# Two attention layers with a bidirectional recurrence: the steps of the recurrence split into five parts and placed by a table

## The reference

```python
x = x + L0_attn(L0_cond(x, fside, fside, w, u, cond), W, g1, g2, g3)
x = x + L0_ffn(L0_cond2(x, fside, fside, w, u, cond), weight, bias)
x = x + L1_attn(L1_cond(x, fside, fside, w, u, cond), w_q, w_k, w_v, w_o)
x = x + L1_ffn(L1_cond2(x, fside, fside, w, u, cond), w1, w2)
```

```python
score = softmax(att, axis=-1) + softmax(att, axis=-2)
```

## Time and profile before

| | us |
|---|---|
| three runs: lowest, median, highest | 426.21, 428.22, 430.42 |
| the profiled execution: its time, and its span | 429.75, 428.0 |
| busy in the span: PE, DVE, ACT, POOL | 275.2, 262.7, 204.8, 47.1 |

### The profile page before, as it was taken

How to read it: one execution, slowest core, us unless ns; L and a number is a source line. 1 busy time by engine, 2 the same in 40 slices (tenths; PEclk the granted TensorE clock), 3 DMA queues, 4 the chain that set the end, 5 groups by cost and what they waited for, 6 DMA issues and landing times.

```text
span 428.0 us, 5935 instructions
## 1 busy us (share of the span) xinstructions
PE 275.2 (64%) x2278; PEld 170.7 (40%) x2278; DVE 262.7 (61%) x502; ACT 204.8 (48%) x333; POOL 47.1 (11%) x76
## 2 busy tenths in 40 slices
PE   0151866694696786737335428898889999755644
PEld 0141433462453353523212314665566666423413
DVE  2977976969669552698858354345456140494762
ACT  3655693865856735412650361551644343233512
POOL 2000111101111100053210502002000000000000
PEclk9996895896987788666658556898985865886986
DMA  5813554333765522022270500000000000000100
GB/s 172 331 31 70 99 100 80 70 74 75 165 131 98 102 50 51 0 49 49 51 147 0 98 0 0 2 2 0 2 2 0 2 2 0 0 2 1 49 27 25
DMA packets 8525, 23.58 MB, mean 55 GB/s; under 512 B 1585, under 2 KB 2993, under 8 KB 8113
## 3 DMA queue, kind: packets, MB, share of 16 engines
q0 software_dynamic: 4320, 15.73, 19.5%
q1 hardware_dynamic: 4176, 7.48, 5.1%
HBM read 6.43 MB, written 1.05 MB: 17 GB/s over the span
## 4 chain that ended last, share of the span: by engine, by line
PE 44%; DVE 27%; ACT 12%; issue 10%; DMA 4%; POOL 2%; DVEq 0%; ACTq 0%; POOLq 0%
PE PS L1224 7%; DVE fwd L649 5%; PE PO L1072 5%; PE PM L1172 4%; PE PM L1112 4%; PE PO L1057 4%; PE PO L1239 3%; PE PM L1028 3%; PE PM L1098 2%; DVE fwd L918 2%; DMA fwd<-mid 2%; DMA fwd<-bwd 2%; DVE bwd L657 2%; PE PM L1181 2%; DVE kp L873 2%
## 5 line engine op out<-in xcount | busy, mean ns | idle before, releaser
L873 DVE TENSOR_REDUCE kp<-PS 128x2 f32<-128x256 f32 x64 | 32.3, 551 | 25.5 <-PE PS L1203 25.4
L558 ACT ACTIVATE E<-PS 128x384 f32<-128x384 f32 x64 | 27.9, 490 | 37.1 <-PE PS L1224 37.0
L482 ACT ACTIVATE E<-PS,negc,escale 128x1024 f32<-128x1024 f32 x32 | 38.3, 1198 | 11.6 <-PE PS L1042 11.4
L1072 PE MATMUL PO<-E,vr 128*32 128x256 f32 x256 | 22.7, 483 | 32.7 <-DVE vr L751 26.4
L1002 PE MATMUL PM<-w,sg 128*128 128x256 f32 x32 | 11.3, 517 | 28.5 <-DVE sg L672 28.5
L460 ACT ACTIVATE yc<-PO 128x256 f32<-128x256 f32 x32 | 12.4, 387 | 30.5 <-PE PO L1057 29.1
L276 POOL DMA_DIRECT2D fwd<-mid x15 | 13.1, 872 | 122.0 <-DVE fwd L649 122.0
L1224 PE MATMUL PS<-TP 32*128 32x256 f32 (+1 forms) x128 | 20.2, 417 | 9.3 <-DVE kp L873 6.0
L1172 PE MATMUL PM<-G,sg 128*128 128x512 f32 x32 | 21.8, 842 | 6.6 <-DVE sg L672 6.5
L1072 PEld LDWEIGHTS PO<-E,vr 128*32 128x32 f32 x256 | 8.0, 126 | 41.5 <-DVE vr L751 37.2
L1028 PE MATMUL PM<-ident,kp 128*128 128x128 f32 x96 | 17.5, 341 | 10.9 <-POOL kp L341 8.8
(11 more groups left out here) (167 smaller groups left out, 626.2 us busy)
## 6 DMA issues: line engine op xcount, KB each, us to landing
fwd<-mid POOLq DMA_DIRECT2D x15, 512.0 KB, 4.5
fwd<-bwd POOLq DMA_DIRECT2D x15, 512.0 KB, 4.5
G<-in_w SPq DMA_DIRECT2D x2, 1024.0 KB, 9.6
kT<-in_kT SPq DMA_DIRECT2D x4, 256.0 KB, 6.6
xT<-in_xT SPq DMA_DIRECT2D x4, 256.0 KB, 6.2
G<-in_attn SPq DMA_DIRECT2D x1, 1024.0 KB, 6.4
out<-ek SPq DMA_DIRECT2D x8, 128.0 KB, 1.7
w<-in_attn SPq DMA_DIRECT2D x1, 512.0 KB, 7.5
```

Of the source, the lines that this page charges most:

```text
L482: nc.scalar.activation(E[:, p % 6], PS[:, 2 * (p % 2):2 * (p % 2) + 2, :], ACT.Exp, bias=negc[:], scale=escale[:]).then_inc(S["e0_done"], 1)
L558: nc.scalar.activation(E[:, p % 4, i, 0:384], PS[:, i, 0:384], ACT.Exp, scale=QSCALE).then_inc(S["e1_done"], 1)
L873: nc.vector.tensor_reduce(kp[:, b % 2, u * H + 2 * j:u * H + 2 * j + 2, D], PS[:, at0:at0 + 2, lo:hi], AX, ALU.max, negate=True).then_inc( ...
L1072: ins = nc.tensor.matmul(PO[SLOT * g:SLOT * (g + 1), 1, at:at + T], vr[:, q % 2, v * 4 + g, :], E[:, (2 * q + g // 2) % 6, g % 2, v * T:(v ...
```

## The change

- **Parts by a table.** Steps 2 to 11 are cut into five parts (`inputs`, two `ahead`, two `behind`), and a slot takes as many parts as `FILL` says, (2, 2, 2, 2, 1, 2, 1, 1) over eight slots. `prepare` is placed two slots before the first part, `wkv` three and `gate` four slots after the last. All ten steps end in slot 29, as they did.
- **Links higher.** `links` comes right after the first part of its slot; in slot 33, where there is none, before `gate(11)`.
- **Preparation of a batch** goes by a small table `PREP`, which differs for batch 1 alone: `project0(1)` moves from slot 1 to slot 2, the rest with it. `turn_y` moves up in its slot.
- **Late steps.** 14 and 15 move on: the parts of step 14 stand at slots -10 (`inputs`), -9 (`ahead`), -7 (`behind`), 5 (`wkv`), 7 (`gate`), those of step 15 at -2, 1, 3, 10 and 12. Step 13 keeps its scans; its `wkv`, with that of step 12, goes from slot -9 to -3. Each late `wkv` is behind a load of the table with the logarithm, and the next tanh loads the other.
- **Ternary weights.** They are loaded a second time, into `ek` and `ekv`, once all scans are done; rounding is in slots 14 and 22 and clipping in slots 16 and 24 of the second attention.
- **Clears.** The clear of `vt` on GpSimd moves to the start of the program, the large one of `kp` to VectorE in slot 34; the small ones stay on GpSimd, now before `add_mid(12)`.
- `cond` is loaded ahead of the first segment of `kT`; `prepare(12)` and `inputs(12)` are in slot 34, ahead of `yT_copy` and of three `gated`.

```diff
-        w1f = G[3][:, :]
-        w2f = G[2][:, :]
+        w1f = ek[:, :]
+        w2f = ekv[:, :]
...
-        M_AT = {n: 3 * (n - RAMP) for n in range(RAMP, BEFORE)}
-        M_AT[BEFORE] = B * PAIRS + 4
-        M_LATE = {BEFORE + i: -17 + 3 * i for i in range(1, B)}
+        FILL = (2, 2, 2, 2, 1, 2, 1, 1)
+        PART_AT = {}
+        for at in range(B * PAIRS):
+            for _ in range(FILL[at % PAIRS]):
+                n, part = divmod(len(PART_AT), 5)
+                if n + RAMP < BEFORE:
+                    PART_AT[n + RAMP, part] = at
+        LATE = {BEFORE + 1: (-14, -13, -12, -3, -1), BEFORE + 2: (-10, -9, -7, 5, 7),
+                BEFORE + 3: (-2, 1, 3, 10, 12)}
+        PREP = {1: 1, 2: PAIRS, 3: 2 * PAIRS}
...
+            sp.wait_ge(S["scan_done"], 4 * LAYERS * B)
+            sp.wait_ge(S["m_done"], LAYERS * B)
+            sp.dma_start(w1f, w1_d).then_inc(S["ld_w1"], 16)
+            sp.dma_start(w2f, w2_d).then_inc(S["ld_w2"], 16)
...
-            pool.wait_ge(S["ktr0_done"], HALF * B)
-            pool.wait_ge(S["y0_done"], B * CH)
-            nc.gpsimd.memset(vt[:, :, :, D:2 * D], 1.0).then_inc(S["v_ones"], 1)
+            pool.wait_ge(S["kp_clear"], 1)
-            link(nc.gpsimd.memset(kp[:, :, :, D:SLOT], 0.0))
...
-                for n in steps0(p, 0):
-                    inputs(n)
-                for n in steps0(p, 1):
-                    if n < BEFORE:
-                        ahead(n, 0)
-                        ahead(n, 1)
-                for n in steps0(p, 2):
-                    if n < BEFORE:
-                        behind(n, 0)
-                        behind(n, 1)
+                for i, (n, part) in enumerate(parts(p)):
+                    if part == 0:
+                        inputs(n)
+                    elif part <= 2:
+                        ahead(n, part - 1)
+                    else:
+                        behind(n, part - 3)
+                    if i == 0 and p % 2 == 1 and 0 <= (p - 3) // 2 < B * CH:
+                        links((p - 3) // 2)
...
+                if p == 34:
+                    dve.wait_ge(S["ktr0_done"], HALF * B)
+                    dve.wait_ge(S["vcols_done"], B * CH)
+                    nc.vector.memset(kp[:, :, :, D:SLOT], 0.0).then_inc(S["kp_clear"], 1)
+                    inputs(BEFORE)
+                    for bb in range(B - 1):
+                        gated(1, bb)
+                        largest(bb)
```

More of the change, by code:

```diff
@@ L197, in build, with parts, steps0, steps1 @@
         BEFORE = 3 * LAYERS
-        LAST = LAYERS * B - 1
-        M_AT = {n: 3 * (n - RAMP) for n in range(RAMP, BEFORE)}
-        M_AT[BEFORE] = B * PAIRS + 4
-        M_LATE = {BEFORE + i: -17 + 3 * i for i in range(1, B)}
-        def steps1(p, lag):
-            return [n for n, at in M_LATE.items() if at + lag == p]
-        def steps0(p, lag):
-            return [n for n, at in M_AT.items() if at + lag == p]
+        FILL = (2, 2, 2, 2, 1, 2, 1, 1)
[8 more added lines that the diff above has]
+        PREP = {1: 1, 2: PAIRS, 3: 2 * PAIRS}
+        def parts(p):
+            return [key for key, at in PART_AT.items() if at == p]
+        def steps0(p, part, lag):
+            return [n for n in range(RAMP, BEFORE) if PART_AT[n, part] + lag == p]
+        def steps1(p, i, lag=0):
+            return [n for n, at in LATE.items() if at[i] + lag == p]
+        def prep(p, lag):
+            return [b for b, at in PREP.items() if at + lag == p]
         def added(n):
@@ L230, in _ @@
         def _(sp):
+            sp.dma_start(cond[:], cond_d.partition_broadcast(P)).then_inc(S["ld_cond"], 16)
             sp.dma_start(kT[:, seg(0)], kT_d[:, seg(0)]).then_inc(S["ld_k0"], 16)
[L232 removed]
             sp.dma_start(vec[:], vec_d).then_inc(S["ld_vec"], 16)
@@ L324, in _ @@
                 link(nc.gpsimd.memset(kp[half[0], :, u * H:(u + 1) * H, at:at + 1], 1.0))
+            add_mid(BEFORE)
             add_back(BEFORE)
@@ L327, in _ @@
                 b, j = p // PAIRS + 2, p % PAIRS
-                for n in steps1(p, 1):
+                for n in steps1(p, 1, 1):
                     add_mid(n)
-                for n in steps1(p, 2):
+                for n in steps1(p, 2, 1):
                     add_back(n)
@@ L486, in _ @@
                     weight_abs(1)
[L487 to L490 removed]
                 if p % 2 == 0 and 0 <= p // 2 - 1 < B * CH:
                     rows_copy(p // 2 - 1, 0, "pv0_done", "turned0_done", "rows0_done")
+                for bb in prep(p, 1):
+                    square0(bb)
+                for bb in prep(p, 3):
+                    rms(bb)
                 if j == 3 and 1 <= b <= B:
                     yT_copy(b - 1, "ytr0_done", "out0_done", "yT0_done", gv[:])
[L495 to L498 removed]
+                for bb in prep(p, 5):
+                    kT_copy(bb, 0)
+                for bb in prep(p, 6):
+                    kT_copy(bb, 1)
                 if p % 4 == 3 and p >= 7 and (p - 7) // 4 < B * HALF:
                     turned_copy((p - 7) // 4)
[L501 to L509 removed]
+                for n in steps0(p, 4, 3):
+                    wkv(n)
+                for n in steps0(p, 0, -2):
+                    prepare(n)
+                if p == 34:
                     for bb in range(B - 1):
                         tanh(1, bb)
+                    prepare(BEFORE)
             tanh(1, B - 1)
@@ L734, in _ @@
             behind(1, 0)
+            behind(1, 1)
             low_parts(0, 0)
-            behind(1, 1)
             low_parts(0, 1)
@@ L800, in _ @@
-                if p == 0:
-                    gate(1)
-                for n in steps0(p, 6):
-                    if n < BEFORE:
-                        gate(n)
-                if j == 0 and b + 1 < B:
-                    gated(0, b + 1)
-                if j == 6 and b + 1 < B:
-                    low_parts(b + 1, 0)
-                if j == 7 and b + 1 < B:
-                    low_parts(b + 1, 1)
-                if p % 2 == 1 and 0 <= (p - 3) // 2 < B * CH:
-                    links((p - 3) // 2)
@@ L813, in _ @@
-                if j == 2 and b + 1 < B:
-                    sums0(b + 1)
-                if p == 34:
-                    for bb in range(B - 1):
-                        gated(1, bb)
-                        largest(bb)
+                for bb in prep(p, 4):
+                    normed(bb)
+                for i, (n, part) in enumerate(parts(p)):
[7 more added lines that the diff above has]
+                        links((p - 3) // 2)
@@ new lines, in _ @@
+                if not parts(p) and p % 2 == 1 and 0 <= (p - 3) // 2 < B * CH:
+                    links((p - 3) // 2)
+                if p == 1:
+                    gate(1)
+                for n in steps0(p, 4, 4):
+                    gate(n)
+                for bb in prep(p, 0):
+                    gated(0, bb)
+                for bb in prep(p, 6):
+                    low_parts(bb, 0)
+                for bb in prep(p, 7):
+                    low_parts(bb, 1)
+                for bb in prep(p, 2):
+                    sums0(bb)
@@ L972, in _ @@
                         rotary(b + 2, u)
-                for n in steps1(p, 6):
+                for n in steps1(p, 4):
                     if n == BEFORE + 1:
@@ L1123, in _ @@
                     scores0(p)
+                if j == 2 and 1 <= b <= B:
+                    turn_y(b - 1, "ytr0_done", [("y0_done", CH * b), ("qT0_done", 4 * min(b + 1, B))])
                 if p % 2 == 0 and 0 <= (p - 4) // 2 < B * CH:
```

74 lines of the change are left out of this document (25 added, 49 removed).

## The result

| | before | after |
|---|---|---|
| three runs: lowest, median, highest (us) | 426.21, 428.22, 430.42 | 395.05, 396.64, 398.34 |
| span of the profiled execution | 428.0 | 394.9 |

The ratio of the medians is 0.926, 95% interval 0.917 to 0.936: 31.6 us faster, where 22 were forecast. The time lies inside the range, near its lower end, and outside the forecast proper (402 to 412). Of four of the experiments (parts spread as before, late steps back, a better lead-in, and the kernel before with links moved up) the profile is of an execution at the upper end of that kernel's times, so from these four only the rows and stages named are read.

A forecast was written before the change was run, and what follows sets the result against it. VectorE was busy longest in the first attention, waits bounded the second's lead-in, TensorE its slots. Terms -15, +0.5, -3.5, -11 and +7 gave -22: median 406 us, forecast proper 402 to 412, range 395 to 419.

The forecast's parts named there:

- Better: Rival: TensorE, held up less, stays at 2.4 GHz for more of the first attention, slots hide nearly all: 397, chance 0.14.
- First attention: Clips leave VectorE, prepare stands a slot earlier, links comes sooner: -15 us, bounds -8 and -22.
- First feed-forward: Clears of vt and kp leave GpSimd, so the one L839 of 4.148 us runs like the others: -3.5 us.
- End of the attention: End of the first attention: the clear on VectorE is covered by waits, prepare(12) holds the last project_both by about 0.5: +0.5 us.
- Lead-in: Lead-in of the second attention: two late chains shorten, work added in slot -3 mostly hidden: -11 us, bounds -8 and -12.5.
- Chain one: Second attention's lead-in: two table loads and two wkv no longer stand ahead of tanh(2, 1); project_qk(1) starts 4.6 us earlier.
- Chain two: Same lead-in: batch 1's additions no longer wait behind step 15's DMA on GpSimd; turn(1, 0) 11.1 us earlier, project_qk(1)'s 4.6 included.
- most is hidden: Slot -3 of the lead-in: prepare(15), a load and two wkv, mostly hidden under the 6.04 us wait before the first scores.
- Slots: Second attention's slots: inserted ScalarE work of 11.6 us costs 5.8, VectorE work of 8.2 costs 1.2: +7 us, bounds +3 and +11.
- The rival that exposes the insertions fully: Second attention's slots pay 19.8 us for the inserted work instead of 7: 419, chance 0.10.
- the slow one: Rival: new holds in the second attention drop TensorE's clock to 1.2 GHz: 439, slower than before, chance 0.03.
- Table loads dearer than their row: Rival: each of the four new ScalarE table loads costs twice its 1.28 us: 411, chance 0.05.

The follow-up runs named there:

- a better lead-in: Changed kernel with wkv(12) and wkv(13) at slot -8, their gates at -6 and inputs(15) at slot -3: 390.56 us, ratio 0.919 to the kernel before.
- chain one undone: Changed kernel with wkv(12) and wkv(13) at slot -9 and their gates at -8 again, step 15 late as changed: 397.47 us, ratio 0.934 to the kernel before.

## Why the prediction was right, and where its sizes were off

- **The waits were forecast at their size; the clock was not.** No term held a change of the clock, so the sum of -22 amounts to 22 us less idle time of TensorE. That idle time fell by 23.1 over the span; the other 9.9 us came off its busy time. The measured 396.64 is what the rival "Better" gave (397, chance 0.14), and for its first reason: TensorE runs at 2.4 GHz for more of the time. Its second reason, that the slots hide nearly all, doesn't hold. That the single terms meet their measured lengths as well as they do is in part luck, as the next points say.
- **First attention: right mechanism, undersized.** The term was -15 and measured -24 and -23.3, beyond its bound of -22. TensorE's idle time accounts for 15.6 of it, its busy time for 8.3. VectorE, from whose rows the term was made, did 4.9 less and waited 19.0 less, and here two steps failed. "Of 13.8 I take 10": the wait for `mid` went wholly, and undoing `prepare` alone cost 7.5 us in time and 10.4 in the stage. "The wait of 12.2 for `project_both` stays": it fell to 7.9 in the first profile and 11.1 in the second, so this is 1 to 4, and unsteady. What the term left out on purpose was the clock: it rose from 0.83 to 0.93, and TensorE's 8.3 us less busy time is nearly all that lies beyond the forecast. The condition that I named as proving it wrong, a granted clock that moves by over 0.05, came about in both attentions: from 34 us to the end of the first it is 0.81 before and 0.87 after (between the links 0.83 and 0.93), in the slots of the second 0.78 and 0.83. That the clock follows from the removed waits was not shown apart; in the table above it goes with the idle time among the variants of the changed kernel (0.93 at 18.4, 0.89 at 24.5, 0.86 at 26.4), but the kernel before had 0.83 at 34.1 and, with links moved up, 0.81 at 24.7.
- **The parts don't add up.** Undone one by one, the place of links, prepare, the spread and the ternary weights cost 14.2, 10.4, 4.0 and 4.9 us in the stage, 33.5 together against 24. In TensorE's idle time they are 8.0, 6.1, 2.4 and 1.5, together 18.0 against 15.6: the waits nearly add up, and most of the excess is busy time at another clock. Links alone gave 7 to 11 us in the kernel before.
- **Ternary weights: -3.7 in the first attention, not contradicted** (4.9, within what that stage scatters), but as a whole the edit is worth nothing.
- **First feed-forward: -3.5, measured -3.7.** The cause was right, but it is the order on GpSimd that counts, not that the clears leave that engine. The Trainium skill, page "SBUF — State Buffer", section "Who interferes with whom", describes the block, and the trace agrees for the clears: the one L839 was held over both, from 185.40 to 189.55. The estimate drawn from it, that the DMA issue of `add_mid(12)` would block as well, doesn't hold here: that issue lasts from 163.46 to 164.53, over the quantisations that start at 163.6, and all four take 0.48 to 0.49.
- **End of the attention: +0.5, measured +1.3 and +1.5.** Without the clear on VectorE it was not shorter (17.6 and 17.7), so it isn't the clear; what it is stays open.
- **Lead-in: -11, measured -13 to -14.** Chain one as forecast (-4.9 for -4.6). Chain two -9.0 beyond it, as against 6.5, but then "most is hidden" was wrong: slot -3 exposes about 3.3 of its work. From the turn to the first scores it takes 17.7 instead of 16.8. The two misses partly cancel, which is luck. Part of chain two came from the one-slot lag of `add_mid`, which I hadn't listed as an edit.
- **Slots: +7, measured +3.** The cost in waits was forecast at its size: TensorE is idle 19.3 us of the stage where it was idle 12.3, 7.0 more, and 3.8 of that are waits for `E`. The length grew by less, since the clock rose from 0.78 to 0.83 and TensorE is busy 98.2 instead of 102.2 us; no term held that. Undone one by one, the late steps give back about 6 of the 7.0 and the ternary weights 1.7. The rival that exposes the insertions fully fell, and so did the slow one, since the clock rose.
- **Table loads dearer than their row: no.** The load at 216.82 ends at 218.10 and tanh begins at 218.11. The figure of 2.66 in the Trainium skill, page "ScalarE: Activation LUTs", section "What ACT_TABLE_LOAD costs", has a drain that these rows don't show.
- **Last feed-forward: a term that was missing.** +2.5 and +2.2, for the same instructions: TensorE is busy 33.96 instead of 30.45 at a clock of 0.77 instead of 0.82, and VectorE 34.78 against 34.79. So the clock has a part in it, but it isn't all: with chain one undone the clock was 0.80, TensorE was busy 31.8, and the stage took 58.8 all the same. Two kernels (parts as before, late steps back) had 56.4 and 56.6, the others built on the changed one 58.4 to 58.8, and the kernel before with links moved up, whose stage is unchanged, 57.9. The cause stays open.

## What to carry to other kernels

When one engine does the links of a critical chain and filler besides, put the links right behind the first piece of filler in their slot and make what the filler reads ready a slot sooner than it seems to need: the two were worth 11 and 6 to 7 us here, and a table of filler parts 4 to 6. Read the idle time and the busy time of the engine that the chain runs through separately: in seven profiles of the same stage its length went from 95.2 to 100.5 us, its idle time only from 18.4 to 19.7. A clear or other filler on a second engine is priced by what it runs beside, so its place in that engine's queue can matter more than which engine does it. Moving work off a crowded stage pays only what the receiving stage hides: look at the other end of the move before counting the gain, as the ternary weights (0 net) and the `wkv` at slot -3 (3.3 of 4.5 paid back) show.
